# A routed language-model tower on one core: the first group's expert logits move from VectorE to GpSimd in the second routing

## The reference, cut to what matters

```
h = tok(x, value)                     # embedding rows + value rows, both normalised
h = h + ssm(norm(h))                  # a long convolution
h = h + moe(norm(h))                  # first experts: 8 experts, 2 of them per token
h = h + attn(norm(h))                 # sampled attention
h = h + hmoe(norm(h))                 # second experts: 8 groups of 8 experts

def hmoe(x):
    logits1 = x @ g1                              # 8 numbers per token
    v1, i1  = top_k(logits1, 2)                   # the two best groups
    c1      = softmax(v1) put at i1
    logits2 = x @ g2[g] for every group g         # 8 x 8 numbers per token
    v2, i2  = top_k(logits2, 2) in every group    # the two best experts of each
    c2      = softmax(v2) put at i2
    y[g, e] = relu(x @ W1[g, e] + b1[g, e]) @ W2[g, e] + b2[g, e]
    return sum over g, e of c1[g] * c2[g, e] * y[g, e]
```

## Time and profile before

| | |
|---|---|
| median of three runs | 1117.53 us |
| lowest, highest | 1114.18, 1117.86 us |
| time of the profiled execution | 1117.68 us |
| its span (first to last instruction) | 1115.9 us |
| busy: PE, DVE, ACT, POOL | 770.6, 780.9, 447.6, 509.8 us |
| granted TensorE clock, mean | 0.753 of full speed |
| second routing up to the pick of group 1 | 680 to 685.7 us of the span |
| the two picks | 685.7 to 695.3 us |
| expert stage of the second experts | 779.5 to 1040 us |

### The profile page before, as it was taken

The page is one execution under the profiler, slowest core; times in us unless marked ns, Lnnn a source line. Parts: engine busy times, 40 slices in busy tenths (PEclk is TensorE's granted clock), DMA queues, the critical chain, the costliest instruction groups (busy, mean ns, idle before and its releaser), DMA issues.

```text
span 1115.9 us, 18090 instructions
## 1 busy us (share of the span) xinstructions
PE 770.6 (69%) x5133; PEld 632.8 (57%) x5133; DVE 780.9 (70%) x2301; ACT 447.6 (40%) x1233; POOL 509.8 (46%) x528
## 2 busy tenths in 40 slices
PE   0206968478999935787776783112999999999352
PEld 0205347358999922444342663011998999999342
DVE  7977273865666535888886667999787776777643
ACT  2555142342444423344320052046565566666210
POOL 7853000135555056556510000035777773777675
PEclk9856985557999965666666565555999999999755
DMA  3193039601222128765562004041344443444223
GB/s 73 41 371 154 1 98 297 217 8 51 73 69 70 42 58 166 136 136 119 126 118 39 1 0 145 0 129 56 102 116 111 116 115 93 123 120 122 74 62 99
DMA packets 116600, 112.95 MB, mean 101 GB/s; under 512 B 16403, under 2 KB 102994, under 8 KB 116258
## 3 DMA queue, kind: packets, MB, share of 16 engines
q1 hardware_dynamic: 103228, 84.68, 27.7%
q0 software_dynamic: 13280, 27.13, 9.7%
HBM read 76.15 MB, written 35.57 MB: 100 GB/s over the span
## 4 chain that ended last, share of the span: by engine, by line
PE 54%; DVE 27%; DMA 7%; POOL 5%; issue 3%; ACT 3%; SPq 0%; DVEq 0%; ACTq 0%; POOLq 0%
PE ps L638 16%; PE ps L645 15%; DVE wide L1348 7%; PE ps L1969 4%; DVE wide L1229 3%; POOL wide L878 3%; PE ps L2139 2%; DMA wide<-results,place 2%; PE ps L2180 2%; PE ps L633 2%; ACT wide L1757 2%; DVE bnst L959 2%; PE ps L2231 1%; POOL wide L814 1%; PE ps L2119 1%
## 5 line engine op out<-in xcount | busy, mean ns | idle before, releaser
L638 PE MATMUL ps<-wide 128*128 (+1 forms) x1580 | 236.5, 281 | 3.5 <-issue 1.5
L645 PE MATMUL ps<-big,wide 128*128 x1568 | 232.1, 278 | 0.0
L638 PEld LDWEIGHTS ps<-wide 128*128 128x128 f32 x1580 | 205.0, 194 | 10.4 <-issue 8.7
L645 PEld LDWEIGHTS ps<-big,wide 128*128 128x128 f32 x1568 | 201.8, 193 | 0.1
L606 ACT ACTIVATE wide<-ps,wide 128x128 f32<-128x128 f32 x395 | 137.3, 366 | 152.4 <-PE ps L638 151.1
L559 DVE TENSOR_SCALAR wide<-ps,wide 128x128 f32<-128x128 f32 x395 | 131.7, 348 | 87.0 <-PE ps L638 80.3
L871 POOL DMA_INDIRECT wide<-xrows,holder x149 | 143.9, 966 | 93.0 <-PE ps L633 58.0
L1348 DVE TENSOR_REDUCE wide<-ps 125x3 f32<-125x1500 f32 (+1 forms) x96 | 143.8, 1541 | 34.8 <-PE ps L1969 34.0
L878 POOL DMA_INDIRECT wide<-results,place x128 | 126.5, 988 | 58.6 <-issue 32.6
L1969 PE MATMUL ps<-big 97*125 97x500 bf16 x256 | 106.4, 553 | 37.7 <-DVE wide L1348 32.3
L550 DVE COPY wide<-big 128x258 f32 (+2 forms) x328 | 109.0, 332 | 19.7 <-issue 18.9
(11 more groups left out here) (386 smaller groups left out, 1197.9 us busy)
## 6 DMA issues: line engine op xcount, KB each, us to landing
results<-wide SPq DMA_DIRECT2D x161, 128.0 KB, 1.8
big<-kappa SPq DMA_DIRECT2D x8, 1750.0 KB, 20.6
big<-parts SPq DMA_DIRECT2D x96, 125.0 KB, 5.4
big<-in_L_ffn_W_dram SPq DMA_DIRECT2D x10, 1024.0 KB, 8.8
big<-in_L_ffn_W_dram SPq DMA_DIRECT2D x64, 128.0 KB, 2.7
parts<-wide SPq DMA_DIRECT2D x24, 250.0 KB, 3.2
xrows<-wide SPq DMA_DIRECT2D x2, 1792.0 KB
wide<-results,place POOLq DMA_INDIRECT x192
```

The source lines that it names most:

```text
L638: last = t.matmul(ps[:, (2 if k < c.HC // 2 else 4) + u % 2, 128 * k:128 * k + 128], ring.w1[u % U][:, 128 * k:128 * k + 128], turned, sta ...
L645: last = t.matmul(ps[:, 6 + u % 2, 0:D], ring.hid[u % 2][:, 128 * k:128 * k + 128], w[:, D * k:D * k + D], start=k == 0, stop=k == c.HC - 1)
```

## The change

The kernel after gives the pick of group 1 to GpSimd, and replaces the three constant semaphores with one counter.

- After the first `top`, VectorE raises `route_out`. It goes on with `without` and the second `top`, and does the pick of group 2. Then it waits for `route_in`, and goes on with the `top` over both groups.
- GpSimd, behind the filling of `chain`, waits for `route_out`, and does the same four instructions on the same shapes: the product over 2048 numbers and the three halvings. It works in `m["slot"]` (in `tbuf`) and leaves the 256 sums in the first half of `m["rest"]`. The last one raises `route_in`. Only then does it come to its wait for `f1_placed`.
- `iota_ready`, `iota2_ready` and `aconst_ready` become `constants_ready`, raised three times by GpSimd in the same order and waited for at 1, 2 and 3.

```diff
+                    m = mask_views(1)
+                    w = m["slot"]
+                    pool.wait_ge(S("route_out"), 1)
+                    me.then(gp.tensor_tensor(out=w.rearrange("p (g e t) -> p g e t", g=8, e=8), in0=m["le"].rearrange("p (g e t) -> p g e t", g=8, e=8),
+                                             in1=m["oh1"][:, 0:256].rearrange("p (g t) -> p g t", g=8).unsqueeze(2).broadcast_to([R, 8, 8, NT]), op=ALU.mult))
+                    me.then(gp.tensor_tensor(out=w[:, 0:1024], in0=w[:, 0:1024], in1=w[:, 1024:2048], op=ALU.add))
+                    me.then(gp.tensor_tensor(out=w[:, 0:512], in0=w[:, 0:512], in1=w[:, 512:1024], op=ALU.add))
+                    gp.tensor_tensor(out=m["rest"][:, 0:256], in0=w[:, 0:256], in1=w[:, 256:512], op=ALU.add).then_inc(S("route_in"), 1)
                 pool.wait_ge(S(q + "placed"), 1)
...
                     top(lg, oh[0], 1, small(0, 1), small(12, 1))
+                    dve.sem_inc(S("route_out"), 1)
                     without(lg, oh[0], flat)
                     top(lg, oh[1], 1, small(1, 1), small(13, 1))
                     rest = v4("rest", 2)
 
-                    for i in range(2):
-                        hot_g = oh[i][:, 0].unsqueeze(2).broadcast_to([R, 8, 8, NT])
-                        me.then(TT(out=tmp, in0=le, in1=hot_g, op=ALU.mult))
-                        over_groups(flat(rest[:, i:i + 1]))
+                    me.then(TT(out=tmp, in0=le, in1=oh[1][:, 0].unsqueeze(2).broadcast_to([R, 8, 8, NT]), op=ALU.mult))
+                    over_groups(flat(rest[:, 1:2]))
+                    dve.wait_ge(S("route_in"), 1)
...
-            gp.memset(alpha[:, 3:4], 0.0).then_inc(S("iota_ready"), 1)
+            gp.memset(alpha[:, 3:4], 0.0).then_inc(S("constants_ready"), 1)
...
-            dve.wait_ge(S("iota2_ready"), 1)
+            dve.wait_ge(S("constants_ready"), 2)
```

More of the change, by code:

```diff
@@ L810, in _ @@
             me.then(gp.iota(ecolI[64:128, :], pattern=[[0, 1]], base=64 - 1 + FFN[1].part_blocks[0], channel_multiplier=1))
-            gp.iota(em8I[:, :], pattern=[[1, 8]], base=-8, channel_multiplier=0).then_inc(S("iota2_ready"), 1)
+            gp.iota(em8I[:, :], pattern=[[1, 8]], base=-8, channel_multiplier=0).then_inc(S("constants_ready"), 1)
             pool.wait_ge(S("ids_ready"), 1)
@@ L840, in _ @@
             gp.affine_select(out=own16, in_=own16, compare_op=ALU.is_ge, fill=0.0, base=DK - 1,
-                             pattern=[[DK, H]], channel_multiplier=-1).then_inc(S("aconst_ready"), 1)
+                             pattern=[[DK, H]], channel_multiplier=-1).then_inc(S("constants_ready"), 1)
             for f in (0, 1):
@@ L1273, in attention_weights @@
                 dve.wait_ge(S("ld_attn"), 16 * 9)
-                dve.wait_ge(S("aconst_ready"), 1)
+                dve.wait_ge(S("constants_ready"), 3)
                 me.did(v.tensor_copy(i500, i500.bitcast(I32)))
@@ L1544, in _ @@
             dve.wait_ge(S("emptied_dve"), nth[at["ssm", 0]])
-            dve.wait_ge(S("iota_ready"), 1)
+            dve.wait_ge(S("constants_ready"), 1)
             me.then(v.tensor_copy(itF[:, :], itI[:, :]))
```

## The result

The changed kernel took 1118.86 us (median of 22 runs), the kernel before 1113.78 us (22 runs). The ratio is 1.0031, with a 95% interval from 1.0016 to 1.0046: slower by 0.31%. The ratio is the one on record with its interval; the two medians alone would give 1.0046, the upper end of that interval. Measured once more beside other runs it was 1.0021 (1.0001 to 1.0040). The profiled execution of the changed kernel has a shorter span than that of before, 1112.0 against 1115.9 us. That is no gain from the change: its routing began 6.3 us earlier (first reduction at 673.73 us against 680.04), behind code that does the same work. So the two traces are compared stretch by stretch, not by their spans.

A forecast was written before the change was run, and what follows sets the result against it. VectorE was taken to bound the second routing: 6.32 us of standing and about 0.03 us of semaphores against 4.78 us removed give +1.6 us, forecast 1119.2 us; the 8-in-10 range is 1115.2 to 1122.2 us.

The forecast's parts named there:

- VectorE sets the end here: Second routing: VectorE is busy nearly without a gap, so a microsecond of VectorE is a microsecond of the kernel.
- They take turns: Second routing: two-SBUF-input VectorE instructions and GpSimd tensor_tensors don't overlap; GpSimd's four hold 7.71 us together.
- they run side by side: Rival, second routing: GpSimd's pick overlaps VectorE's work, gaining 3.6 us, to 1114.0 us; chance 0.12.
- What is hidden: Second routing: only VectorE's two reductions, 0.58 us each, and the overheads overlap with GpSimd's work.
- GpSimd's durations: GpSimd's pick: 4.47, 2.33, 1.26 and 0.73 us for its four instructions, sum 8.79, bounds 7.94 and 9.58.
- The sum, +1.6 us: Second routing: 6.32 us of standing and about 0.03 us of semaphores against 4.78 us of pick removed.
- The semaphore: VectorE's signal and its already met wait in the second routing: about 0.03 us in the sum.
- Who is first: After the signal: L1023 runs first, 682.66 to 683.08, then GpSimd's 2048 numbers hold the turn until 687.28.
- What hides: Second routing: the first reduction runs beside GpSimd's 2048 numbers, the second beside its 512; each takes 0.58 us.
- What would show it: New trace: L1026 and L1027 take some 4.0 and 2.4 us, reductions stay 0.58, the wait for `route_in` is empty.
- The expert stage: Rival: TensorE's granted clock rises earlier or later against the work, worth some 2 us, 1117 or 1121; chance 0.10.
- The higher price: Rival, second routing: whole-duration holds, standing reductions or a slower broadcast product make it +2.6 to +4.5 us; chance 0.20.

The follow-up runs named there:

- One more product: The kernel before with the product of the first group done twice on VectorE; stretch 2.33 us longer, ratio 1.0024.
- the version with one SBUF input: The changed kernel with first best removed before the signal and VectorE operands partly in PSUM, so none reads two SBUF inputs; ratio 0.9989, again 0.9950.
- GpSimd only writes: The changed kernel with GpSimd's four pick instructions replaced by six memsets, the first group's pick left out; stretch 8.14 us, ratio 0.9962.
- the kernel in which VectorE waits at once: The changed kernel with VectorE's wait for GpSimd moved directly behind its signal, so nothing overlaps; stretch 17.07 us, ratio 1.0042.
- The three versions with PSUM: The changed kernel with at most one SBUF input on VectorE, traced twice (0.9989, 0.9950), and that version with the last halving back on VectorE (0.9973).
- the counter only: The kernel before with only its three constant semaphores made one counter; stretch 12.65 us, ratio 0.9990.
- GpSimd writing beside: VectorE picks both groups as in the kernel before, with the counter, while GpSimd runs six memsets beside it; stretch 12.79 us, ratio 1.0007.

## Why the prediction held, point by point

- **VectorE sets the end here.** Right. One more product added 2.33 us to the stretch and 1.0024 came out. Ten of the eleven intervals in the table hold the ratio that the stretch gives; the second measurement of the version with one SBUF input is the exception, by 0.7 thousandths.
- **They take turns.** Right, and it is what decided the sign: without the turns (GpSimd only writes, for some 8 us) the kernel is 0.38% faster, with them 0.2 to 0.3% slower. The rival "they run side by side" would have had L1026 at 0.42 us; it took 1.82.
- **What is hidden.** Right: the reductions, and beyond them only GpSimd's starts, ends and gaps. All of it is 2.38 us, the difference to the kernel in which VectorE waits at once.
- **GpSimd's durations.** 4.47, 2.33, 1.26, 0.73 us were worked out from the rows of 128 and 512 numbers; 4.50, 2.34, 1.26 and 0.72 were measured where nothing met them. The slope through the row of 1000 numbers, whose second operand is bf16, would have been 0.67 us short for the first. One sum in the prediction is off: 8.79 us is that of the four instructions alone, and with 0.06 us between them it is 8.97; the bounds of 7.94 and 9.58 lack the gaps too. From first start to last end 9.05 us were measured, with gaps of 0.07 to 0.08. The forecast doesn't hang on it, since its steps count the gaps, but the rival "they run side by side" would have gained 3.4 us and not 3.6.
- **The sum, +1.6 us.** 0.47 us too small: 1.57 as worked out, 2.04 in the trace. Three terms of it. *The semaphore*: `sem_inc` and the met wait were put at 0.03 us; the signal cost 0.12 us over the usual gap (676.29 to 676.44, where a gap is 0.03). At the met wait for `route_in` the gap was 0.03 us (690.95 to 690.98), the usual one again. *Who is first*: by the prediction L1023 would have run before GpSimd's first. With the delay of the signal it came 0.01 us behind it (676.44 against 676.43), and stood for 4.35 us. So the hold was 4.36 us from GpSimd's start to 0.14 us before its end, and not 4.20: the 0.14 us taken off at the start, from the earlier trace rows, weren't there. The prediction's own rows had shown such a meeting and it wasn't used for this: L1316 started 0.04 us behind L891, and at its usual 0.35 us it stood from its start on the earlier trace rows. Where GpSimd is the one that waits, the 0.14 us hold: L858 starts 0.20 us before L1032 ends and takes 2.40 us instead of 2.34. *What hides*: by the changed order the second reduction fell beside GpSimd's 256 numbers, with a hold of 0.46 us, instead of the 512 with 0.99, and hid 0.22 us less in all (7.87 us of hold less 6.70 of standing is 1.17 us; predicted were 7.71 less 6.32, 1.39). The sum is: 4.35 + 1.40 + 0.95 us of standing and 0.12 are 6.82, less 4.78 is 2.04.
- **What would show it.** The picture was right, the sizes by row weren't. L1026 and L1027 were to take some 4.0 and 2.4 us and took 1.82 and 1.37, because it was L1032, put at 0.42, that stood for the whole product. VectorE's product of 2048 numbers took its plain 2.29 us and not a little over. GpSimd's took 4.50, 2.40, 1.32 and 0.79 us (4.7, 2.4, 1.35 and 0.8 were said). The reductions stayed at 0.58 to 0.59, VectorE didn't idle at `route_in`, and the rest of the way differs by 0.4 us.
- **The expert stage.** The rival in which it gives or takes some 2 us didn't come between these two traces: from the list of rows to its last product it takes 262.4 us before and 262.6 after.
- **The higher price.** The rival with whole durations for holds had 4 x 0.27 = 1.08 us more than the 1.57 worked out, 2.65; 2.04 was measured, between them. The first hold ended 0.14 us before GpSimd's end (L1032's own 0.42 us began at 680.79, L856 ended at 680.93). The reductions didn't stand, 0.58 to 0.60 us beside tensor_tensor and memset alike, and with memsets in GpSimd's place the stretch was 12.79 us.
- **The time.** 1119.2 us was predicted and 1118.86 measured, but by luck: the kernel before came out at 1113.78 us in 22 runs and not at the 1117.53 of the three shown. From 1113.78 the same sum gives 1115.4, 3.5 us under what was measured. The predicted 1.6 us are 0.14% and the measured ratio is 0.31% (0.16 to 0.46), at the edge between "the same", which got 0.65, and "slower", which got 0.22. The stretches say 0.18%.

## What to carry to other kernels

An idle GpSimd was not free help for VectorE here. Ask of each pair that would run together whether the VectorE instruction reads two tiles in SBUF and the GpSimd one is a tensor_tensor on tiles in SBUF. Such pairs took turns here (0.42 us of VectorE's work took 4.77, 1.82 and 1.37), and GpSimd's 2.2 ns for a number of an f32 tensor_tensor (4.50 us for 2048) were added to a chain that would have done it at 1.1 (2.29 us). (A GpSimd instruction that reads a single tile wasn't tried.) Work that did overlap here is VectorE's reductions (0.58 to 0.59 us beside a tensor_tensor), its instructions with one operand in PSUM (0.43 us), and GpSimd's memsets (0.42 us for the first instruction beside them); moving one operand of each VectorE instruction to an empty PSUM bank, behind a signal raised one instruction later, turned +2.04 us into -2.83 here.

In a trace look at the duration of one instruction against its twins elsewhere, not at busy shares: the standing L1032 counts as busy for all of its 4.77 us.

## What the runs showed of the hardware that was not expected

- A VectorE instruction with two SBUF inputs that starts 0.01 us after a long GpSimd one stands for all of it but 0.14 us: 0.42 us of work took 4.77 us, in three traces alike (4.77, 4.76, 4.76).
- The part ahead of the second routing scatters far more than the changes measured here. In twelve profiles with the same code up to there (the three constant semaphores aside) its first reduction starts between 671.66 and 680.39 us. The first expert stage's first product starts between 256.0 and 260.1 us, so some of the scatter is there by then. What makes it was not tried.
- The expert stage of the second experts, from the list of rows to its last product, took 261.9 to 264.1 us in the twelve traces; the routing from the reduction over both groups to that list took 84.0 to 84.4. The three versions with PSUM are at 263.3 to 264.1, the others at 261.9 to 263.6. TensorE's granted clock rises from 0.50 to 1.00 in the first microseconds of the stage (in the kernel before 0.50 from 784 to 786 us, 0.96 from 786 to 788 and 1.00 from 790 to 792), not always at the same place: with the counter only its mean is 0.68 already 3 to 5 us behind the list, with GpSimd writing beside it is 0.50 up to 7 us, and those two stages took 262.9 and 263.6 us. But the kernel before had 0.54 at 5 to 7 us and took 262.4, so the rise alone doesn't order the stages. What makes them scatter by 2 us was not tried.
- VectorE instructions with an operand in PSUM were no slower: 0.43 us for 256 numbers and 1.22 for 1024, where it is 0.42 to 0.43 and 1.22 to 1.23 from SBUF. A reduction of 256 numbers from PSUM to PSUM took 0.43 us, where 0.58 is the time from SBUF; from SBUF to PSUM it was 0.60, so the difference goes with the input.
- A bare `sem_inc` between two dependent VectorE instructions put 0.12 us between them beyond the usual 0.03 (676.29 to 676.44 in the change).
